# Maximum pairs laid over half steps by width, the divisions half a step apart, and the floor as a column of part_max

## What is computed

```python
att = jnp.einsum('bhqd,bhkd->bhqk', q, k) / np.sqrt(HEAD_DIM)
att = jnp.where(causal, att, 0.0)
att = jax.nn.softmax(att, axis=-1)
out = jnp.einsum('bhqk,bhkd->bhqd', att, v)
```

## Time and profile before

| | us |
|---|---|
| median of 3 runs | 1168.41 (1167.45 to 1170.62) |
| the profiled execution | 1168.67 |
| its span, from the first instruction to the last | 1166.9 |
| tokens | to 231.8 |
| groups 0 to 7, first exp to first exp | 232.0, 344.9, 459.9, 572.5, 685.2, 797.8, 910.7, 1023.2 |

### The profile page before, as it was taken

The page is one execution under the profiler, slowest core; times in us unless marked ns, Lnnn a source line. Parts: engine busy times, 40 slices in busy tenths (PEclk is TensorE's granted clock), DMA queues, the critical chain, the costliest instruction groups (busy, mean ns, idle before and its releaser), DMA issues.

```text
span 1166.9 us, 21937 instructions
## 1 busy us (share of the span) xinstructions
PE 1102.6 (94%) x8192; PEld 564.3 (48%) x8192; DVE 856.9 (73%) x1185; ACT 712.9 (61%) x1519; POOL 383.3 (33%) x945
## 2 busy tenths in 40 slices
PE   5999999899999999999999999999999999999888
PEld 3665555454544444444444444445454445444435
DVE  4568776478778877887888788868986897788112
ACT  2433333267775777677667767775777677767552
POOL 3211211344423442433344144314431444142301
PEclk9999999989997999899989999998999899989999
DMA  3575753490029002800460055006400830020123
GB/s 124 171 260 172 209 163 125 156 136 9 7 29 128 6 7 35 122 6 6 51 106 6 6 67 90 6 6 82 78 2 7 96 65 7 2 81 8 42 73 113
DMA packets 53390, 83.61 MB, mean 72 GB/s; under 512 B 6308, under 2 KB 36260, under 8 KB 49572
## 3 DMA queue, kind: packets, MB, share of 16 engines
q1 hardware_dynamic: 52132, 78.01, 31.9%
q0 software_dynamic: 1152, 4.19, 1.2%
HBM read 43.78 MB, written 33.55 MB: 66 GB/s over the span
## 4 chain that ended last, share of the span: by engine, by line
PE 61%; DVE 9%; ACT 5%; issue 4%; ACTq 0%; DVEq 0%
PE ps_s L1133 21%; PE ps_o L1147 21%; PE ps_m L287 8%; DVE part_max L304 7%; ACT probs L1004 5%; PE ps_o L1157 3%; PE ps_m L1179 3%; PE ps_m L294 2%; PE ps_s L1122 2%; PE ps_s L1112 1%; DVE normed L1051 1%; PE ps_s L1123 1%; DVE turned L1040 1%; ACT shift_t L985 1%; ACT sums L991 0%
## 5 line engine op out<-in xcount | busy, mean ns | idle before, releaser
L304 DVE TENSOR_REDUCE part_max<-ps_m 128x2 f32<-128x1024 f32 (+1 forms) x598 | 615.8, 1061 | 161.6 <-PE ps_m L287 117.4
L1004 ACT ACTIVATE probs<-ps_s 128x512 f32<-128x512 f32 (+3 forms) x1280 | 590.0, 539 | 202.2 <-PE ps_s L1133 195.0
L1133 PE MATMUL ps_s<-q_op,k_op 50*128 50x512 f32 (+3 forms) x1280 | 449.6, 429 | 21.0 <-ACT probs L1004 10.1
L287 PE MATMUL ps_m<-k_op,q_op 48*128 48x512 f32 (+3 forms) x1196 | 348.3, 419 | 19.4 <-DVE part_max L304 18.4
L1133 PEld LDWEIGHTS ps_s<-q_op,k_op 50*128 50x128 f32 x1280 | 214.5, 190 | 285.4 <-ACT probs L1004 208.1
L952 POOL TENSOR_SCALAR_AFFINE_SELECT probs<-probs 128x128 f32<-128x128 f32 x512 | 145.2, 292 | 501.0 <-ACT probs L1004 492.3
L1147 PE MATMUL ps_o<-probs,v_sb 128*32 128x512 f32 (+3 forms) x2560 | 305.4, 550 | 0.0
L287 PEld LDWEIGHTS ps_m<-k_op,q_op 48*128 48x128 f32 x1196 | 173.8, 191 | 51.5 <-DVE part_max L304 46.6
L919 POOL TENSOR_TENSOR diag_weight<-ident,masked_weight 128x256 f32<-128x256 f32 x256 | 147.6, 612 | 54.6 <-ACT masked_weight L971 54.6
L294 PE MATMUL ps_m<-mask,pick 64*128 64x64 bf16 (+1 forms) x936 | 97.1, 212 | 0.0
L1147 PEld LDWEIGHTS ps_o<-probs,v_sb 128*32 128x32 f32 x2560 | 51.1, 109 | 72.2 <-issue 36.2
(11 more groups left out here) (82 smaller groups left out, 768.0 us busy)
## 6 DMA issues: line engine op xcount, KB each, us to landing
parts_d<-parts SPq DMA_DIRECT2D x32, 512.0 KB, 4.7
q_op<-parts_d SPq DMA_DIRECT2D x42, 256.0 KB, 14.0
k_op<-parts_d SPq DMA_DIRECT2D x42, 256.0 KB, 16.1
vpad_d<-v_pad SPq DMA_DIRECT2D x32, 256.0 KB, 3.4
v_sb<-vpad_d SPq DMA_DIRECT2D x8, 1024.0 KB, 7.7
x_in<-x SPq DMA_DIRECT2D x8, 512.0 KB, 5.4
ffn_d<-ffn SPq DMA_DIRECT2D x8, 512.0 KB, 3.1
attn_t<-normed SPq DMA_DIRECT2D x128, 32.0 KB, 2.0
```

Source lines behind the costliest of these rows:

```text
L287: last = pe.matmul(ps_m[:, f % ring * 2 + e, 0:width], self.q_op[rows, p, j, q0:q0 + P], self.k_op[rows, p, j, pc * CH:pc * CH + width], s ...
L304: dve.tensor_reduce(both, ps_m[:, bank:bank + 2, 0:width], AX_X, ALU.max).then_inc(self.piece_reduced, 1)
L1004: act.activation(probs[:, slot % PRING, 0:width], ps_s[:, bank_of("scores", slot, first, last), 0:width], ACT.Exp).then_inc(probs_ready, 1)
L1133: pe.matmul(ps_s[:, bank_of("scores", slot, first, last), 0:CH - q0], k_op[rows, p, h % 2, kt * P:(kt + 1) * P], q_op[rows, p, h % 2, u * ...
```

## The change

1. Pieces are no longer one to a half step. `spread_pieces` gives each half step room CH + 2 x (its queries) and each piece a load of 64 + its width, and puts a piece into the half step in which the middle of its load falls. A half step takes none, one or two pieces. `HEAD_START` becomes 44 (two more pieces in the token stage, two fewer in the last group).
2. The norm steps lie behind score indices 9, 11, 13 and 15.
3. `floor` is gone: `part_max` has a buffer for each unit and one column more, zero from a memset (LOWEST for the last query), so the first max step takes the floor along. There are three max steps instead of four, and the second is a tensor_scalar.

```diff
-HEAD_START = PIECES - 2 * AHEAD_FROM
+HALVES = 2
-MAX_STEPS = 4
+MAX_STEPS = 3
+def spread_pieces():
+    halves = [(u, kt, half) for u in range(NCH) for kt in range(key_tiles(u)) for half in range(HALVES)]
+    halves = halves[AHEAD_FROM * HALVES:] + halves[:AHEAD_FROM * HALVES]
+    room = [CH + 2 * (CH - first_query(u, kt)) for u, kt, _ in halves]
+    load = [P // 2 + piece(f)[4] for f in range(PIECES)]
+    behind = [sum(load[:f]) + load[f] // 2 for f in range(PIECES)]
+    until = [sum(room[:k + 1]) for k in range(len(halves))]
+    at = [next(k for k in range(len(halves)) if behind[f] * until[-1] < until[k] * sum(load)) for f in range(PIECES)]
+    return {where: [f for f in range(PIECES) if at[f] == k] for k, where in enumerate(halves)}
...
-        self.floor = sb("floor", [P, GH, NT])
-        self.part_max = sb("part_max", [P, 2, GH * SUB, NCH])
+        self.part_max = sb("part_max", [P, NCH, GH * SUB, NCH + 1])
...
         if k == 0:
             dve.wait_ge(self.piece_reduced, reduced + MRING)
-            dve.tensor_reduce(self.raw_max[:].rearrange("p h s -> p (h s)"), self.part_max[:, u % 2, :, 0:u + 1], AX_X,
-                              ALU.max).then_inc(self.raw_ready, 1)
+            dve.tensor_reduce(self.row_max[:, u].rearrange("p h s -> p (h s)"), self.part_max[:, u, :, 0:u + 2], AX_X,
+                              ALU.max).then_inc(self.max_ready, 1)
         if k == 1:
-            dve.wait_ge(self.raw_ready, n + 1)
-            dve.scalar_tensor_tensor(self.row_max[:, u], self.raw_max[:], 1.0, self.floor[:, :, u * SUB:(u + 1) * SUB],
-                                     ALU.mult, ALU.max).then_inc(self.max_ready, 1)
+            dve.wait_ge(self.max_ready, n + 1)
+            dve.tensor_scalar(by_head[0].bitcast(F32R), self.row_max[:, u], -1.0, None, ALU.mult).then_inc(self.hi_ready, 1)
         if k == 2:
-            dve.wait_ge(self.max_ready, n + 1)
-            dve.scalar_tensor_tensor(by_head[0].bitcast(F32R), self.row_max[:, u], -1.0, self.floor[:, :, 0:SUB],
-                                     ALU.mult, ALU.add).then_inc(self.hi_ready, 1)
-        if k == 3:
             dve.wait_ge(self.hi_ready, n + 1)
...
-                        f, ahead = piece_at(u, hs // GH, hs % GH // 2)
+                        some, ahead = pieces_at(u, hs // GH, hs % GH // 2)
...
-                        if NORM_AT <= hs < NORM_AT + NORM_STEPS and not (first and u == 0):
+                        norm, between = divmod(hs - NORM_AT, HALVES)
+                        if 0 <= norm < NORM_STEPS and not between and not (first and u == 0):
...
-                            f, ahead = piece_at(u, kt, at // 2)
+                            some, ahead = pieces_at(u, kt, at // 2)
                             if at % 2 == 0 and not (ahead and last):
...
+                                for f in some:
...
+                                    ops.score_piece(pe, ps_m, MRING, f, 1 - p if ahead else p, (G + ahead) * PIECES)
```

More of the change, by code:

```diff
@@ L83, in piece, with key_tiles, first_query, pieces_at @@
     return u, j, s, pc, (CH if pc < u else P * (s + 1))
+def key_tiles(u):
+    return SUB * (u + 1)
+def first_query(u, kt):
+    return P * max(0, kt - SUB * u)
+def spread_pieces():
[7 more added lines that the diff above has]
+    return {where: [f for f in range(PIECES) if at[f] == k] for k, where in enumerate(halves)}
+SPREAD = spread_pieces()
+HEAD_START = sum(len(SPREAD[u, kt, half]) for u, kt, half in SPREAD if KT0[u] + kt >= AHEAD_FROM)
+def pieces_at(u, kt, half):
+    return SPREAD[u, kt, half], KT0[u] + kt >= AHEAD_FROM
 def score_uses(first, last):
@@ L108, in rows_of @@
     return slice(h // 2 * HALF, h // 2 * HALF + rows)
-def piece_at(u, kt, half):
-    ahead, f = divmod(HEAD_START + 2 * (KT0[u] + kt) + half, PIECES)
-    return f, ahead
 def pieces_beside_tokens(n, step):
@@ L122, in pieces_beside_tokens @@
     return range(until(n * TOKEN_STEPS + step), until(n * TOKEN_STEPS + step + 1))
-def key_tiles(u):
-    return SUB * (u + 1)
-def first_query(u, kt):
-    return P * max(0, kt - SUB * u)
 def build(nc, x, w_in_t, w_r_t, w_k_t, w_v_t, w_out_t, mu_rk, out):
@@ L199, in set_constants @@
         pool.memset(self.pick16[:], 0.0).then_inc(self.consts_set, 1)
-        pool.memset(self.floor[:], 0.0).then_inc(self.consts_set, 1)
+        pool.memset(self.part_max[:], 0.0).then_inc(self.consts_set, 1)
         pool.memset(self.after[:, NT - 1], 0.0).then_inc(self.consts_set, 1)
@@ L216, in set_constants @@
         pool.wait_ge(self.consts_made, 9)
-        pool.affine_select(out=self.floor[:, :, NT - 1], in_=self.floor[:, :, NT - 1], compare_op=ALU.not_equal, fill=LOWEST,
+        floor = self.part_max[:, NCH - 1].rearrange("p (h s) c -> p h s c", s=SUB)[:, :, SUB - 1, NCH]
+        pool.affine_select(out=floor, in_=floor, compare_op=ALU.not_equal, fill=LOWEST,
                            base=-(P - 1), pattern=[[0, GH]], channel_multiplier=1).then_inc(self.consts_made, 1)
@@ L1193, in group @@
                             score_tile(u, kt, at, i, p, first, last)
-                            f, ahead = piece_at(u, kt, at // 2)
+                            some, ahead = pieces_at(u, kt, at // 2)
                             if at % 2 == 0 and not (ahead and last):
-                                if ahead and f == 0:
-                                    pe.wait_ge(q_loaded[1 - p], ops.loaded(1 - p, i + 1 + p))
-                                    pe.wait_ge(k_loaded[1 - p], ops.loaded(1 - p, i + 1 + p))
-                                ops.score_piece(pe, ps_m, MRING, f, 1 - p if ahead else p, (G + ahead) * PIECES)
+                                for f in some:
+                                    if ahead and f == 0:
+                                        pe.wait_ge(q_loaded[1 - p], ops.loaded(1 - p, i + 1 + p))
+                                        pe.wait_ge(k_loaded[1 - p], ops.loaded(1 - p, i + 1 + p))
+                                    ops.score_piece(pe, ps_m, MRING, f, 1 - p if ahead else p, (G + ahead) * PIECES)
                             if at == GH - 1:
```

11 lines of the change are left out of this document (5 added, 6 removed).

## The result

The changed kernel takes **1209.07 us** (median of 4 runs, 1205.64 to 1216.51) against 1168.8 us for the kernel before on the same chip (4 runs, 1167.45 to 1170.62). The ratio is 1.0352, 95% interval 1.0300 to 1.0404: slower by 3.5%. The profiled execution is the longest of the four, 1216.51 us, 47.8 more than that of before.

| execution | us | mean granted clock |
|---|---|---|
| before, profiled | 1168.67 | 0.972 |
| changed | 1205.64 | 0.972 |
| changed | 1207.40 | 0.972 |
| changed | 1210.73 | 0.969 |
| changed, profiled | 1216.51 | 0.963 |

A forecast was written before the change was run, and what follows sets the result against it. No engine is full: each slot is a closed loop of PE and ACT. Group and token terms add 18.7 us to 1168.67, giving 1187.4; the clock's 9.2 makes 1196.6, with 8 in 10 for 1150 to 1214.

The forecast's parts named there:

- Slot as a closed loop, second piece paid in full: Wide slots: PE and ACT wait on each other; a late second piece costs 0.6 us, none given back.
- The triples' prices: Slots with three pieces: the last waits for the first's reduce, 1.13 us if wide; 8.85 us a group.
- Slot 4: Three pieces at the start of unit 1: 1.13 us, with DVE some 0.3 late, so 1.4.
- The losses of before: Waits for DVE in today's group: about 6.3 us of 112.7, of which 4.1 in slots 4 to 6.
- The clock: TensorE's clock falling around slot 4: 0 to 8 falls at 2.3 us, half taken, +9.2 us.
- Group 7: Last group, pieces in slots 0 to 18 only: loses 2.9 us instead of 6.1, so -3.2.
- Norm steps: Spaced half a step apart: the reduce of 73 comes sooner, removing the 0.6 us of slots 16 and 17.
- Head start 44: Two pieces more in the token stage, each between nothing and a reduce of 1.22 us: +1.3 us.
- Rival 1: Narrow slots' relief wins as three-piece slots hide their wait: 1131 us, half hidden about 1150; chance 0.19.
- rival 2: It comes out even, three-piece slots costing 0.75 us with the clock up: 1165 to 1172 us; chance 0.09.
- Rival 3: The clock falls also behind wide three-piece slots 20, 27, 33, 36: some 1238 us; chance 0.04.
- Rival 4: Pieces are not where counted, so slots 27, 33, 36 lack three; time either side; chance 0.02.

The follow-up runs named there:

- the run with one triple: The kernel before with one piece moved from slot 32 to slot 31, which then has three pieces: 1178.42 us, ratio 1.0086.
- the run with light triples: The kernel before with new norm steps and floor, three three-piece slots starting 128 wide, one piece each in slots 1, 2, 3: 1161.62 us.

## Why the prediction was right, and where it wasn't

The profiled executions differ by +47.8 us: tokens +1.6, group 0 +8.2, group 1 +3.7, groups 2 to 6 +28.8, group 7 +5.6. The medians differ by +40.3, and the prediction's sum was +27.9. The sign and the mechanism were right, and 1209 lies inside the range of 1150 to 1214. The size was a third short: 12 us above the 1196 of the sum, and 1 us above the 1208 where the likeliest case ended.

**Slot as a closed loop, second piece paid in full: held.** The row of slot 33 is at +2.38, the very figure worked out from the earlier trace rows, and in the run with one triple the slot behind gave nothing back.

**The triples' prices: held**, nearly all a little high. With the slot behind included: slots 27, 33 and 36 came to 1.05, 1.01 and 1.03 us (1.13 predicted), slot 0 to 0.82 (0.9), slots 19 to 21 to 1.88 (1.95), slot 24 to 0.62 (0.6), slot 13 to 0.27 (0.45); slots 9 to 11 are 0.5 faster where 0.15 was charged. Slots 0 to 3 came out even (9.9), as 0.9 for the triple against 0.8 of relief had it. Slots 8 to 39 lost 4.7 us a group where these terms, less what was to go away there, made 5.25.

**Slot 4: under-sized, and this is the first term that failed.** 1.4 us was the price; PE's weight load waited 1.99 us (the longest of its kind). The rows of group 2:

```profile
482.69 0.50 PE L1144 MATMUL ps_s<-q_op,k_op 50*128 50x512 f32 x1
482.77 4.79 POOL L928 TENSOR_TENSOR diag_weight<-ident,masked_weight 128x256 f32<-128x256 f32 x8
482.78 0.88 DVE L1055 TENSOR_TENSOR turned<-turned,inv_denom 128x256 f32<-128x256 f32 x1
483.70 0.71 DVE L1060 STREAM_TRANSPOSE normed<-turned 128x512 f32<-128x512 f32 x1
484.34 1.52 DVE L318 TENSOR_REDUCE part_max<-ps_m 128x2 f32<-128x1024 f32 x2
485.58 0.29 PEld L301 LDWEIGHTS ps_m<-k_op,q_op 48*128 48x128 f32 x2 [1.99 <-DVE part_max L318]
486.18 0.62 PE L1144 MATMUL ps_s<-q_op,k_op 50*128 50x512 f32 x1
```

The first reduce starts 1.65 us after the slot (482.69), not 0.77 + 0.3, and the fourth score tile at 486.18, +3.49 where 1.4 us of price had it at +2.65: two parts of the norm step stand ahead of it, and the product takes 0.88 us where it takes 0.42 elsewhere, beside GpSimd's eight products. The Trainium skill (SBUF — State Buffer, SBUF: two separate sides) says that an operation of VectorE with two inputs in SBUF and one of GpSimd that reads SBUF lock each other out of a shared pair of ports for a whole instruction. The 0.46 us more is less than one of GpSimd's, 0.60 us, so the row agrees. What counts is when it starts: here 0.01 us into one of GpSimd's operations. With the norm steps alone it starts 0.57 us into one (464.87 in group 2, GpSimd's from 464.30) and takes 0.41, and then GpSimd's next takes 0.88; with the layout alone it has ended before they begin (0.43 at most). The run with light triples has the 0.88 too, and slot 4 takes 3.06 us there: the delay costs something only where a third piece waits behind it.

**The losses of before: held, but the change recovered none of those in unit 1.** That 4.1 us a group lay in slots 4 to 6 is shown by the run with light triples (slots 4 to 7 from 15.5 to 11.55). With the changed kernel they take 15.9.

**The clock: the step that decided the size.** I took half of 0 to 18.4 us, on the ground that one stall of 1.4 us is much like those of before. Before, too, the clock fell in every group from group 1 on, so "much like before" was an argument for a fall in each, not for half. The sum with all eight falls was 1205.8 (1203.5 with the seven that came), within 4 us of the median and within 2 of the two runs whose mean clock is 0.972. Such closeness is in part luck: the sum has slot 4 too cheap and a gain in group 7 that didn't come, and against them 5.25 us a group for the 4.7 of slots 8 to 39. In group 0 the +8.2 stand beside a predicted +7.5, and 2.0 of them are slots 2 and 3 run at 0.50, which no term had. What the profiled run has beyond the sum is second falls (groups 3 and 6, where slots 4 to 7 are 1.2 and 1.5 us over the others and PE's weight loads stand 1.14 and 1.63 us on issue in slot 6), those at slot 1, and the one in slots 20 to 22 of group 7. The Trainium skill (TensorE: Matmul & The Clock Gate, What's actually happening) gives the low state to an idle engine, and by that rule it would have been 1187; the earlier trace rows had spoken against it, and here a stretch with PE busy 1.82 of 3.44 us was followed by 0.50.

**Group 7: wrong sign.** Predicted -3.2. Slots 0 to 18, the only ones with pieces, rose by 1.3: slot 4 is as dear there as elsewhere, the relief in unit 1 didn't come, and slot 2 is 1.3 us longer at a low clock. The other 4.3 are the low stretch of slots 20 to 22.

**Norm steps: right, and small; floor: nothing,** as said. The norm steps' 0.6 us a group is found (0.5 in slots 16 and 17), and is 3.6 us in all.

**Head start 44:** +1.6 us of tokens for +1.3, though the token stage has a low stretch of 3.4 us that the token stage of before hasn't, so the pieces' own share isn't known.

**The rivals.** Rival 1 (the relief wins) needed triples below 0.75 us and rival 2 (it comes out even) needed 0.75; both fell at 1.0. Rival 3 (falls behind wide triples) is not wholly wrong: in the run with the new layout alone the clock fell for 3.4 us in slot 20 of groups 3, 4 and 5, behind the triples of slots 19 and 20, and in the changed kernel in one group. Behind slots 33 and 36 it fell in neither trace; in the changed kernel:

```profile
569.00:572.42 3.42, 2.70 (x24) 1.28 (x16) 2.56 (x3) 2.33 (x5) 0.00 (x0) 1.00 0.00 0
580.00:583.42 3.42, 2.57 (x22) 1.30 (x22) 2.06 (x3) 2.17 (x5) 0.88 (x3) 1.00 0.01 4
```

Rival 4 fell at once: all nine triples stood where they were counted.

**The signs to look for:** by its score tiles slot 33 takes 3.70 us for the 3.8 forecast (counted from exp's end to exp's end it is 3.4, and the rest stands in the slot behind); PE's wait for DVE 1.04 us for 1.3; slots 16 and 17 plain, 2.67 each; PE's waits for `part_max` 73.6 / 8 = 9.2 us a group for "about 9". DVE's busy time is 1.2 us less in group 3 and 12 us less in all, a little outside the 1 us a group. Slots 5 and 6 were plain in none of groups 1 to 7, for the clock fell in each.

## What to carry to other kernels

Even load in the sum isn't even load in the ring: where a buffer ring holds two, the third item of a step waits for the first one's consumer, and the engine's own queue behind it waits too. So lay out work by the order of releases, put the small item first in a crowded step, and leave steps crowded by other work alone; issuing the third item later moves its wait but doesn't remove it. When a stall stands where the clock already falls today, count the fall in every repetition (here it came in seven of seven groups); and when a stretch gets shorter, look at what transfers end in it.
